# Second attention of a six-stage model: output projection of batch 0 inside its loop, first norm's statistics in the experts' tail, fewer split passes, score stacks filled from SBUF

## The chip, the cores and the metric

The kernel runs on one core of a Trainium2 chip. The metric is the device time of one execution in microseconds (us). The core has five engines with queues of their own: TensorE (PE, with its weight loads as PEld), VectorE (DVE), ScalarE (ACT), GpSimd (POOL) and SyncE (SP), which here only issues DMAs.

## The reference

Six residual steps on x[2, 1024, 128] in f32. The change touches the seams of the fifth, the attention of layer 1, with the fourth and the sixth, which are mixtures of experts:

```python
x = x + 0.5 * _L1_ffn_ref(_layernorm(x), gate_w, Wg, Wu, Wd, Sg, Su, Sd)   # experts, "moe0"
x = x + _L1_attn_ref(_layernorm(x), W_qkv, b_qkv, W_proj, b_proj)         # attention, 16 heads of 8
x = x + 0.5 * _L1_ffn_ref(_layernorm(x), gate_w, Wg, Wu, Wd, Sg, Su, Sd)   # experts, "moe1"

# _L1_attn_ref
scores = q @ k.T / sqrt(8) + slopes[:, None, None] * minimum(idx[None, :] - idx[:, None], 0)
y = softmax(scores) @ v
return y @ W_proj + b_proj
# _L1_ffn_ref: logits = flat_x @ gate_w.T; each of 16 experts takes its 256 best tokens
```

## The kernel before, in words

The 2048 tokens stand as 16 tiles of 128 (a quarter is 4 tiles, one PSUM bank of 512 columns). Every stage is a block in which each engine runs a list written by hand; engines meet through semaphores, and a barrier ends the block. `renew()` clears the semaphores between stages and adds a second barrier.

**Tail of moe0.** The experts' results are scattered with adds into two tensors in DRAM. DVE adds the first to XB (L1254), then the second, quarter by quarter as it comes back (L1258), which gives X. Then comes the barrier.

**Prologue of the attention.** DVE takes mean and variance of 16 tiles (L84, L87), ACT one square root, DVE normalises 16 tiles (L143), PE transposes them and ACT keeps them as XT. PE projects q and k, for batch 0 and then batch 1 (`n` = 0 to 3, L1691). Each projection is split into three bf16 parts, high, middle and low: ACT writes it twice (to F and as the high part, L1594), DVE makes the rest, the middle and the low part (L1622 to L1626). SP sends the parts to DRAM (`keep`, L1517) and reads them back into stacks of rows (`part_rows`, L1502 and L1508): KS and QS, [128 rows, 3 stacks, 4 heads, 1024] in bf16. Rows 0 to 71 are parts, 72 to 119 the bias rows (`first_rows`, `bias_rows`), two more the rows' maxima. A stack serves one step `s`, that is one group of 4 heads and one batch. PE also makes the values V, which DVE copies with the bias.

**The loop.** First 48 chunks (`LEAD`) of raw scores go to PE (L1712), and DVE takes the maximum of each (L1635). Then come 128 units `gu`. Each has four score matmuls (L1727), four more chunks for the maxima of a later step, while there are any (512 in all, so until unit 115), ACT's two exponentials (L1606), on the diagonal a multiplication on POOL (L1578), and the product with the values (L1743). Every 8 units half a step ends: its maxima are split into two rows (L1649, L1651), which SP writes into the stack with 8 small DMAs (`maxima`, L1526), and PE waits for them in `z.mrows`; its outputs are turned and normalised into Y.

**The end.** After the loop a block of its own turns Y, projects it and adds it to X; the stage of moe1 then makes the norm (L84 to L160) and the gate's logits (L1267), and DVE's first step on the logits is L1155.

## Time and profile before

| what | us |
|---|---|
| median of 3 runs (1349.92 to 1354.03) | 1349.97 |
| the profiled execution, its own time | 1347.04 |
| its span, first to last instruction | 1345.3 |
| PE busy in it | 1170.4 |
| DVE busy | 851.5 |
| ACT busy | 697.2 |
| POOL busy | 513.6 |

Times inside the execution count from the start of the span. The mean granted clock of TensorE is 0.922 of its full 2.4 GHz. A row of the timeline gives start, length, engine, line, operation, output and inputs, the number of instructions, and in brackets the idle time before it and what ended it. An f32 matmul of 512 columns shows as two records.

### The profile page before, as it was taken

What the parts mean: (1) busy time and instruction counts of PE and PEld (TensorE: products, weight loads), DVE (VectorE), ACT (ScalarE), POOL (GpSimd) and SP (SyncE); (2) the same over time, 40 slices, a digit from 0 to 9 for tenths busy, and PEclk for the clock granted to TensorE, in tenths of its full rate; (3) what the DMA queues carried; (4) which work ended last, traced back from release to release, by engine and by line L of the source; (5) the groups of instructions that cost most, each with busy time, mean ns of one, the idle gap of its engine ahead of it and who ended that gap; (6) DMA issues with size and microseconds to landing.
All of it is one profiled execution on the core that took longest, in us unless ns stands there. A gap on an engine that the chain in (4) does not pass through costs nothing. (4 is left out here: it accounts for less than half of the span.)

```text
span 1345.3 us, 18773 instructions
## 1 busy us (share of the span) xinstructions
PE 1170.4 (87%) x6259; PEld 579.2 (43%) x6259; DVE 851.5 (63%) x1880; ACT 697.2 (52%) x857; POOL 513.6 (38%) x513
## 2 busy tenths in 40 slices
PE   3899999999999977599458999999999998577884
PEld 1444444444444843499431222222222222446874
DVE  6266576666656467633378788888888880684321
ACT  3577778777788143132140566666666666221221
POOL 0056566665657102278500131231131131034774
PEclk9699999999999977799775899999999999597997
DMA  2000010100101105167568020320220000312662
GB/s 80 1 6 24 25 30 22 32 22 22 38 16 33 33 1 191 19 166 187 107 150 157 5 38 12 48 39 10 48 44 5 1 1 5 129 32 70 169 159 20
DMA packets 57099, 73.89 MB, mean 55 GB/s; under 512 B 21162, under 2 KB 45614, under 8 KB 55214
## 3 DMA queue, kind: packets, MB, share of 16 engines
q1 hardware_dynamic: 42876, 63.91, 18.4%
q0 software_dynamic: 11264, 8.92, 4.6%
q8 instruction: 40, 0.66, 0.2%
q10 hardware_dynamic: 2888, 0.15, 0.1%
q14 instruction: 31, 0.25, 0.1%
HBM read 59.68 MB, written 12.98 MB: 54 GB/s over the span
## 5 line engine op out<-in xcount | busy, mean ns | idle before, releaser
L1635 DVE TENSOR_REDUCE at_MX<-psum 128x1 f32<-128x512 f32 x512 | 318.3, 682 | 60.0 <-PE psum L1712 60.0
L1606 ACT ACTIVATE at_PR<-psum 128x1024 f32<-128x1024 f32 x256 | 251.5, 1022 | 178.3 <-PE psum L1727 178.0
L1578 POOL TENSOR_TENSOR at_PR<-at_PR,at_FAC 128x512 f32<-128x512 f32 x64 | 81.0, 1266 | 344.9 <-ACT at_PR L1606 344.9
L1712 PE MATMUL psum<-at_KS,at_QS 120*128 120x512 bf16 x512 | 205.8, 404 | 7.4 <-DMA at_KS<-at_parts_dram 6.3
L1727 PE MATMUL psum<-at_QS,at_KS 122*128 122x512 bf16 x512 | 192.6, 386 | 4.8 <-DMA at_QS<-at_MR 4.3
L515 ACT ACTIVATE PR<-psum 128x1024 f32<-128x1024 f32 x144 | 140.9, 1026 | 82.2 <-PE psum L799 77.8
L520 ACT ACTIVATE PR<-PR 128x1024 f32<-128x1024 f32 x144 | 144.5, 1062 | 0.0
L799 PE MATMUL psum<-Q,K 64*128 64x512 f32 (+3 forms) x768 | 143.5, 502 | 1.2 <-ACT PR L515 1.2
L1743 PE MATMUL psum<-at_PR,at_VG 128*32 128x512 f32 x1024 | 136.2, 604 | 9.5 <-ACT at_OTS L1600 4.7
L811 PE MATMUL psum<-PR,V 128*64 128x512 f32 (+3 forms) x768 | 139.7, 495 | 0.1
L492 POOL TENSOR_SCALAR_AFFINE_SELECT PR<-PR 128x256 f32<-128x256 f32 (+1 forms) x112 | 57.7, 529 | 173.8 <-ACT PR L520 173.7
L1359 PE MATMUL psum<-moe_XGT,moe_WE 128*128 128x256 f32 x512 | 120.3, 389 | 0.0
L1236 DVE TENSOR_TENSOR moe_H<-moe_GL,psum 128x512 f32<-128x512 f32 x64 | 44.0, 687 | 115.1 <-ACT moe_GL L1131 115.1
L1727 PEld LDWEIGHTS psum<-at_QS,at_KS 122*128 122x128 bf16 x512 | 48.9, 98 | 154.7 <-ACT at_PR L1606 96.3
L1359 PEld LDWEIGHTS psum<-moe_XGT,moe_WE 128*128 128x128 f32 x512 | 98.1, 197 | 12.8
L799 PEld LDWEIGHTS psum<-Q,K 64*128 64x128 f32 x768 | 64.2, 186 | 78.5 <-issue 62.6
L1712 PEld LDWEIGHTS psum<-at_KS,at_QS 120*128 120x128 bf16 x512 | 50.4, 99 | 88.6 <-DVE at_MX L1635 54.2
L1080 POOL DMA_INDIRECT moe_XG<-moe_rows_dram,moe_IDX x64 | 63.5, 993 | 60.4 <-DMA moe_IDX<-moe_LS 41.5
L811 PEld LDWEIGHTS psum<-PR,V 128*64 128x64 f32 x768 | 47.0, 136 | 85.3 <-issue 75.3
L1131 ACT ACTIVATE moe_GL<-psum 128x512 f32<-128x512 f32 x64 | 38.2, 597 | 86.1 <-PE psum L1359 86.1
L434 POOL TENSOR_TENSOR ACC<-ACC,PR 128x128 f32<-128x128 f32 (+3 forms) x64 | 71.5, 1117 | 5.3 <-POOL PR L492 1.0
L434 DVE TENSOR_TENSOR XN<-XN,PR 128x128 f32<-128x128 f32 (+3 forms) x64 | 60.4, 943 | 17.6 <-POOL PR L492 16.7
(222 smaller groups left out, 1546.8 us busy)
## 6 DMA issues: line engine op xcount, KB each, us to landing
moe_WE<-in_c_We SPq DMA_DIRECT2D x32, 768.0 KB, 4.3
XB<-at_r_dram SPq DMA_DIRECT2D x32, 256.0 KB, 3.8
at_QS<-at_parts_dram SPq DMA_DIRECT2D x24, 192.0 KB
at_KS<-in_c_krows SPq DMA_DIRECT2D x8, 384.0 KB
at_parts_dram<-at_SPL SPq DMA_DIRECT2D x12, 256.0 KB, 2.5
moe_rows_dram<-XNS SPq DMA_DIRECT2D x2, 1152.0 KB, 9.0
at_KS<-at_parts_dram SPq DMA_DIRECT2D x16, 128.0 KB
at_QS<-at_MR SPq DMA_DIRECT2D x128, 1.0 KB
```

Of the source, the lines that this page charges most:

```text
L434: eng.tensor_tensor(into, old, PR[second[0]][:, h, second[1]:second[1] + w], ALU.add).then_inc(done, 1)
L515: act.activation(PR[u][:, :, :], S[(b + u) % 2][:, :, :], ACT.Tanh, scale=SCALE0 / CLAMP).then_inc(z.clamped, 1)
L520: act.activation(PR[u][:, :, :], PR[u][:, :, :], ACT.Exp, scale=CLAMP).then_inc(z.exped, 1)
L799: mm = pe.matmul(S[(b + u) % 2][:, h, at:at + w], K[row[h], b, j * P:(j + 1) * P], Q[row[h], b, q:q + w], start=True, stop=True)
L811: mm = pe.matmul(O[row[h], q:q + w], V[:, b, j, row[h]], PR[u][:, h, at:at + w], start=(u < 2), stop=(u >= NU - 2), skip_group_check=True)
L1359: mm = pe.matmul(ps[4 + 2 * m + h][:, j * CAP:(j + 1) * CAP], WE[:, e % DEEP, at:at + P], XGT[:, e % 2, :], start=True, stop=True)
L1578: pool.tensor_tensor(pr, pr, FAC[:, 4 * (s // 2):4 * (s // 2) + 4, :], ALU.mult).then_inc(z.factored, 1)
L1606: act.activation(PR[:, gu % PRS, 2 * r:2 * r + 2, :].rearrange("p h n -> p (h n)"), g.psum[:, 2 * r * BANK:(2 * r + 2) * BANK], ACT.Exp).t ...
L1635: dve.tensor_reduce(MX[:, 4 * (r // 2 % 4) + r // 8, r % 2:r % 2 + 1], bank(("max", c))[:, :], AX, ALU.max).then_inc(z.reduced, 1)
L1712: pe.matmul(bank(("max", c))[:, :], QS[0:MROW, t, h, I * P:(I + 1) * P], KS[0:MROW, t, h, khalf * BANK:(khalf + 1) * BANK], start=True, st ...
L1727: mm = pe.matmul(ps[h][:, :], KS[0:KALL, t, h, J * P:(J + 1) * P], QS[0:KALL, t, h, half * BANK:(half + 1) * BANK], start=True, stop=True)
L1743: mm = pe.matmul(O[32 * h:32 * h + 32, :], VG[:, s % 2, J, h, :], PR[:, gu % PRS, h, :], start=(J == 0), stop=(J == BT - 1), skip_group_ch ...
```

## The change

1. In moe0's tail PE adds the two parts with identity matmuls in PSUM; DVE takes the statistics from PSUM quarter by quarter, ACT copies X and takes the roots, all before the barrier. The prologue starts with the normalisation, shared by DVE and ACT.
2. Each projection is written once by ACT (high part) and once by DVE (the rest, from PSUM); ACT makes the middle part. The factor of q goes into the weights. V's bias is added by POOL.
3. The trip through DRAM is gone. For each part and side, three DMAs of 8 rows each fill the stack from SPL: 18 per step in place of 8 (with the one of the bias rows 19 in place of 9). The stack of step 1 is asked for after the first chunk.
4. Maxima rows go out before the next stack's rows; for the first half ACT issues four of the eight.
5. Output projection, bias, addition and statistics of quarters 0 to 2 are put behind units 117, 119, 124 and 126; the last quarter, the norm and the logits follow the loop in the same block. moe1 starts with its logits made, after `renew()`.

```diff
+                if lanes == 2:
+                    act.activation(MX[:, 0:1], g.eps[:, 0:1], ACT.Sqrt).then_inc(z.table, 1)
+                    for k in range(4):
+                        act.wait_ge(s.stats, 4 * k + 4)
+                        act.activation(g.X[:, 4 * k:4 * k + 4, :].rearrange("p t d -> p (t d)"), ps[4 + k], ACT.Copy
+                                       ).then_inc(z.kept, 1)
+                        norm_root(act, g, s, k)
...
                     for k in range(4):
...
+                        dve.wait_ge(z.resummed, k + 1)
+                        norm_stats(dve, g, s, k, ps[4 + k])
+                        if k:
+                            norm_inverse(dve, g, s, k - 1)
+                    norm_inverse(dve, g, s, 3)
...
+                if lanes == 2:
+                    pe.wait_ge(z.added, 1)
+                    for k in range(4):
+                        pe.matmul(ps[4 + k], g.ident[:, :], g.XB[:, 4 * k:4 * k + 4, :].rearrange("p t d -> p (t d)"),
+                                  start=True, stop=False, skip_group_check=True)
+                    for k in range(4):
+                        pe.wait_ge(z.reloaded[k], 16)
+                        pe.matmul(ps[4 + k], g.ident[:, :], LAST[:, 4 * k:4 * k + 4, :].rearrange("p t d -> p (t d)"),
+                                  start=False, stop=True, skip_group_check=True).then_inc(z.resummed, 1)
...
-STACK_DMAS, STACK_FIRST = 9, 2
+STACK_DMAS, STACK_FIRST = 19, 2
...
+FIRST_OUT, SECOND_OUT = 117, 124
...
+        last_row, last_out = bank(("row", HALVES - 1)), bank(("out", HALVES - 1))
+        proj_bank = [last_out, last_row, last_row, last_row]
+        yturn_bank = [last_out, last_row, last_out, ps[3]]
...
+        def maxima_rows(eng, hs, k):
+            t, half = hs // 2 % STACKS, hs % 2
+            eng.wait_ge(z.msplit, hs + 1)
+            for h in range(4):
+                eng.dma_start(QS[MROW + k:MROW + k + 1, t, h, half * BANK:(half + 1) * BANK].rearrange("o (i n) -> o i n", n=P),
+                              MR[4 * h:4 * h + 4, k, :]).then_inc(z.mrows, 16)
...
                 def part_rows(s):
                     q, b, t = s // 2, s % 2, s % STACKS
...
+                    for k, ready in enumerate((y.high, y.mid, y.split)):
+                        for side, into in enumerate((QS, KS)):
+                            n = 2 * b + side
+                            sp.wait_ge(ready, n + 1)
+                            for r in range(PARTS):
+                                row = PROWS * r + DH1 * (k if side == 0 else (k - r) % PARTS)
+                                sp.dma_start(into[row:row + DH1, t, :, :], SPL[q::QUADS, n, k, :]).then_inc(z.stacks[t], 16)
...
-                for n in range(3):
-                    keep(n)
-                sp.wait_ge(y.kept[0], 2 * 16 * PARTS)
+                first_rows(0)
+                bias_rows(0)
+                sp.dma_start(WP[:, :], g.i["c_Wproj"]).then_inc(y.out, 16)
+                sp.dma_start(HB[:, :], g.i["c_bproj"].partition_broadcast(P)).then_inc(y.out, 16)
                 part_rows(0)
-                keep(3)
-                sp.wait_ge(y.kept[1], 2 * 16 * PARTS)
+                sp.wait_ge(z.maxed, 1)
+                first_rows(1)
+                bias_rows(1)
                 part_rows(1)
                 sp.dma_start(FAC[:, :, :], g.i["c_factor"]).then_inc(z.factors, 16)
                 first_rows(2)
                 bias_rows(2)
-                part_rows(2)
                 for hs in range(HALVES):
                     s = hs // 2 + 2
-                    if hs % 2 and hs >= 3 and s < STEPS1:
+                    maxima_rows(sp, hs, 0)
+                    if hs:
+                        maxima_rows(sp, hs, 1)
+                    if hs == 0:
+                        part_rows(2)
...
+                    if gu % UNITS == 5 and 0 < s <= 4:
+                        pool.wait_ge(y.out, 32)
+                        pool.tensor_tensor(g.X[:, 4 * s - 4:4 * s, :], g.X[:, 4 * s - 4:4 * s, :],
+                                           bcast(HB[:, :].unsqueeze(1), [P, 4, D]), ALU.add).then_inc(z.biased, 1)
...
+                def high(n):
                     act.wait_ge(y.projected, n + 1)
...
+                    act.activation(SPL[:, n, 0, :], g.psum[:, PJ[n] * BANK:(PJ[n] + 2) * BANK], ACT.Identity,
+                                   bias=bq[:, n % 2:n % 2 + 1]).then_inc(y.high, 1)
+                def middle(n):
+                    act.wait_ge(y.rest, n + 1)
+                    act.activation(SPL[:, n, 1, :], F[:, n % 2, :], ACT.Copy).then_inc(y.mid, 1)
...
+                normalised(1)
+                for k in range(2):
+                    norm_keep(act, g, s_, k, ps[k])
+                normalised(3)
+                act.wait_ge(y.bscaled, 2)
+                high(0)
+                norm_keep(act, g, s_, 2, ps[0])
+                high(1)
+                middle(0)
+                norm_keep(act, g, s_, 3, ps[1])
+                middle(1)
+                values(0)
+                high(2)
+                middle(2)
+                values(1)
+                high(3)
+                middle(3)
+                values(2)
+                values(3)
+                act.activation(OTS[:, 0, 0:1], g.eps[:, 0:1], ACT.Exp).then_inc(y.table, 1)
...
+                for k in range(3):
+                    norm_root(act, g, last_norm, k)
                 take(HALVES - 1)
+                norm_apply(act, g, last_norm, 2, g.XNS)
+                act.wait_ge(z.yturned, 4)
+                act.activation(g.XT[:, 3 * BANK:], ps[3], ACT.Copy).then_inc(z.yt_last, 1)
+                norm_keep(act, g, last_norm, 0, ps[0])
+                norm_keep(act, g, last_norm, 1, ps[1])
+                norm_root(act, g, last_norm, 3)
+                norm_keep(act, g, last_norm, 2, ps[0])
+                act.activation(OTS[:, 0, 0:1], g.eps[:, 0:1], ACT.Exp).then_inc(z.table, 1)
+                norm_keep(act, g, last_norm, 3, ps[1])
...
+                def rest(n):
+                    dve.wait_ge(y.high, n + 1)
+                    wait(dve, y.split, n - 1)
+                    dve.scalar_tensor_tensor(out=F[:, n % 2, :], in0=g.psum[:, PJ[n] * BANK:(PJ[n] + 2) * BANK],
+                                             scalar=bq[:, n % 2:n % 2 + 1], in1=SPL[:, n, 0, :], op0=ALU.add,
+                                             op1=ALU.subtract).then_inc(y.rest, 1)
+                def low(n):
+                    dve.wait_ge(y.mid, n + 1)
+                    dve.tensor_tensor(SPL[:, n, 2, :], F[:, n % 2, :], SPL[:, n, 1, :], ALU.subtract).then_inc(y.split, 1)
+                normalised(0)
                 dve.wait_ge(y.loaded, 48)
+                dve.tensor_scalar(W[:, 0:D], W[:, 0:D], SCALE1, None, ALU.mult).then_inc(y.bscaled, 1)
                 dve.tensor_scalar(bq[:, 0:1], bq[:, 0:1], SCALE1, None, ALU.mult).then_inc(y.bscaled, 1)
...
+                normalised(2)
+                for b in range(2):
+                    for n in (2 * b, 2 * b + 1):
+                        rest(n)
+                    for n in (2 * b, 2 * b + 1):
+                        low(n)
...
+                    if gu == FIRST_OUT:
+                        keep_y(0)
+                        keep_y(1)
+                    elif gu == FIRST_OUT + 2:
+                        add_out(0)
+                        add_out(1)
+                        last_stats(0)
+                        last_stats(1)
+                    elif gu == SECOND_OUT:
+                        keep_y(2)
+                    elif gu == SECOND_OUT + 2:
+                        add_out(2)
+                        last_stats(2)
+                for k in range(3):
+                    norm_inverse(dve, g, last_norm, k)
                 normalise(HALVES - 1)
+                for k in range(2):
+                    norm_apply_vector(dve, g, last_norm, k, g.XNS)
+                add_out(3)
+                last_stats(3)
+                norm_inverse(dve, g, last_norm, 3)
+                norm_apply_vector(dve, g, last_norm, 3, g.XNS)
...
+                turn_norm(0)
+                turn_norm(1)
+                pe.wait_ge(y.loaded, 48)
+                pe.wait_ge(y.bscaled, 1)
+                project(0)
+                project(1)
+                turn_norm(2)
+                values(0)
+                turn_norm(3)
+                project(2)
+                project(3)
+                for k in range(1, 4):
+                    values(k)
...
-                pe.wait_ge(y.high, 4)
...
+                pe.wait_ge(y.rest, 4)
                 pe.wait_ge(y.varea, NT // 4)
+                pe.wait_ge(y.out, 32)
                 for c in range(4 * LEAD):
...
+                    if gu == FIRST_OUT:
+                        pe.wait_ge(z.normed, HALVES - 2)
+                        pe.wait_ge(z.reduced, CHUNKS1)
+                        pe.wait_ge(z.msplit, HALVES)
+                        turn_y(0)
+                        turn_y(1)
+                    elif gu == FIRST_OUT + 2:
+                        project_out(0)
+                        project_out(1)
+                    elif gu == SECOND_OUT:
+                        pe.wait_ge(z.normed, HALVES - 1)
+                        pe.wait_ge(z.added, 1)
+                        turn_y(2)
+                    elif gu == SECOND_OUT + 2:
+                        pe.wait_ge(z.added, 2)
+                        project_out(2)
                 multiply(last)
+                pe.wait_ge(z.yt, 3)
                 turn_out(HALVES - 1)
...
+                pe.wait_ge(z.exped, 2 * STEPS1 * UNITS)
+                pe.wait_ge(z.normed, HALVES)
+                turn_y(3)
+                norm_turn(pe, g, last_norm, 0, g.XNS, ps[0])
+                pe.wait_ge(z.added, 3)
+                project_out(3)
+                norm_turn(pe, g, last_norm, 1, g.XNS, ps[1])
+                logits(0)
+                norm_turn(pe, g, last_norm, 2, g.XNS, ps[0])
+                logits(1)
+                pe.wait_ge(last_norm.xt, 2)
+                norm_turn(pe, g, last_norm, 3, g.XNS, ps[1])
+                logits(2)
+                logits(3)
...
         stage_alibi_attention(nc, g, sem)
-        stage_experts(nc, g, sem, "moe1", out, False)
+        renew()
+        stage_experts(nc, g, sem, "moe1", out, True)
```

SP's list in the prologue of the attention, before: the parts go to DRAM (L1517), come back into stack 0 (L1502, L1508), and the last of them follow.

```order
L1517 DMA at_parts_dram<-at_SPL 32x4x1024 x9
L1502 DMA at_QS<-at_parts_dram 24x4096
L1508 DMA at_KS<-at_parts_dram 24x4096
L1502 DMA at_QS<-at_parts_dram 24x4096
L1508 DMA at_KS<-at_parts_dram 16x4096
L1508 DMA at_KS<-at_parts_dram 8x4096
L1502 DMA at_QS<-at_parts_dram 24x4096
L1508 DMA at_KS<-at_parts_dram 8x4096
L1508 DMA at_KS<-at_parts_dram 16x4096
L1517 DMA at_parts_dram<-at_SPL 32x4x1024 x3
```

Now, from the first rows of stack 0 to the first of stack 1 (L1489 to L1493 are the bias rows):

```order
L1489 DMA at_QS<-in_c_qrows 48x4096
L1490 DMA at_KS<-in_c_mones 2x4096
L1493 DMA at_KS<-in_c_krows 48x4096
L1512 DMA at_WP<-in_c_Wproj 128x128
L1513 DMA at_HB<-in_c_bproj 128x128
L1505 DMA at_QS<-at_SPL 8x4x1024 x3
L1505 DMA at_KS<-at_SPL 8x4x1024 x3
L1505 DMA at_QS<-at_SPL 8x4x1024 x3
L1505 DMA at_KS<-at_SPL 8x4x1024 x3
L1505 DMA at_QS<-at_SPL 8x4x1024 x3
L1505 DMA at_KS<-at_SPL 8x4x1024 x3
L1489 DMA at_QS<-in_c_qrows 48x4096
```

A stack's 72 rows of each side, which came in 8 transfers of 8, 16 or 24 rows, come in 18 transfers of 8 rows.

PE's list from the last units of the loop to moe1's first transposes, before:

```order
L1727 MATMUL psum<-at_QS,at_KS 128x512 x4
L1743 MATMUL psum<-at_PR,at_VG 32x512 x12
L1751 MATMUL psum<-ident,at_OTS 128x128 x4
L1487 UNCONDITIONAL_BRANCH
L1795 UNCONDITIONAL_BRANCH
L1800 MATMUL psum<-ident,at_Y 128x128 x16
L1807 MATMUL psum<-at_WP,XT 128x128 x16
L1784 UNCONDITIONAL_BRANCH
L1261 UNCONDITIONAL_BRANCH
L160 MATMUL psum<-ident,XNS 128x128 x16
L1267 MATMUL psum<-gate,XT 128x16 x16
```

And now, from the projection of quarter 2 behind unit 126 to the block's end (L1847 is the turn of the outputs, L1862 that of Y, L126 the norm's):

```order
L1872 MATMUL psum<-at_WP,XT 128x128 x4
L1839 MATMUL psum<-at_PR,at_VG 32x512 x8
L1847 MATMUL psum<-ident,at_OTS 128x128 x4
L1862 MATMUL psum<-ident,at_Y 128x128 x4
L126 MATMUL psum<-ident,XNS 128x128 x4
L1872 MATMUL psum<-at_WP,XT 128x128 x4
L126 MATMUL psum<-ident,XNS 128x128 x4
L1880 MATMUL psum<-gate,XT 128x16 x4
L126 MATMUL psum<-ident,XNS 128x128 x4
L1880 MATMUL psum<-gate,XT 128x16 x4
L126 MATMUL psum<-ident,XNS 128x128 x4
L1880 MATMUL psum<-gate,XT 128x16 x8
```

Behind the loop a quarter of the projection is left on PE, and the norm's transposes and the logits stand between its pieces.

## Rows read from the trace of the kernel before

**Rows 1.** Windows: stretches (us), busy time per engine, clock, DMA share, GB/s.

```profile
674.54:712.26 37.72, 17.65 (x64) 11.52 (x65) 23.65 (x66) 13.63 (x15) 2.41 (x4) 0.73 0.68 162
712.26:744.25 31.99, 28.58 (x49) 5.05 (x50) 29.61 (x52) 0.00 (x0) 0.00 (x0) 0.50 0.73 135
1107.66:1137.99 30.33, 25.81 (x161) 5.92 (x157) 1.75 (x7) 22.41 (x24) 5.09 (x4) 1.00 0.00 1
1137.99:1166.01 28.02, 17.01 (x96) 15.09 (x96) 12.07 (x60) 7.43 (x11) 4.51 (x1) 0.71 0.30 118
```

**Rows 2.** Timeline, end of moe0 and start of the attention, DVE.

```profile
666.16 2.29 DVE L1254 TENSOR_TENSOR XB<-XB,X 128x2048 f32<-128x2048 f32 x1 [10.32 <-DMA X<-moe_sum_dram]
...
671.88 1.49 DVE L1258 TENSOR_TENSOR X<-moe_SG,XB 128x512 f32<-128x512 f32 x2 [1.09 <-DMA moe_SG<-moe_spare_dram]
674.59 0.87 DVE L84 BATCH_NORM_STATS2 stats<-X 128x6 f32<-128x128 f32 x4 [1.21 <-PEq L1841]
```

**Rows 3.** Timeline, f32 matmuls of 512 columns in moe1, PE.

```profile
1171.37 2.06 PE L1282 MATMUL psum<-XT,SGU 128*128 128x512 f32 x2
...
1178.20 1.96 PE L1282 MATMUL psum<-XT,SGU 128*128 128x512 f32 x4
```

**Rows 4.** Windows around the end of moe0 and the projections (columns as in Rows 1).

```profile
655.00:668.00 13.00, 0.19 (x2) 0.00 (x1) 2.45 (x3) 0.00 (x0) 5.57 (x4) 0.62 0.54 106
679.00:684.00 5.00, 4.10 (x16) 2.98 (x17) 4.51 (x18) 1.97 (x4) 0.00 (x0) 0.50 1.03 182
684.00:692.00 8.00, 7.35 (x16) 3.08 (x16) 3.00 (x3) 4.72 (x5) 0.00 (x0) 0.91 0.40 64
```

**Rows 5.** DMA issues of the prologue: count, KB each, us to landing.

```profile
at_bv<-in_c_bv SPq DMA_DIRECT2D x1, 64.0 KB, 5.2
```

**Rows 6.** Timeline, prologue of the attention to its first units.

```profile
675.42 0.42 SPq L1531 DMA_DIRECT2D at_bv<-in_c_bv  x1
...
687.72 1.10 ACT L1594 ACTIVATE at_SPL<-psum,at_bq 128x1024 bf16<-128x1024 f32 x1
...
712.26 19.91 PE L1712 MATMUL psum<-at_KS,at_QS 120*128 120x512 bf16 x34 [6.31 <-DMA at_KS<-at_parts_dram]
...
734.26 5.11 SPq L1526 DMA_DIRECT2D at_QS<-at_MR  x8
...
744.25 1.89 PE L1727 MATMUL psum<-at_QS,at_KS 122*128 122x512 bf16 x4 [2.78 <-DMA at_QS<-at_MR]
```

**Rows 7.** Timeline, front stage's norm and logits and moe0's first step.

```profile
500.86 1.65 ACT L111 ACTIVATE XNS<-X,shift,rdev 128x128 f32<-128x128 f32 x4 [0.32 <-DVE shift L103]
500.96 1.11 DVE L118 TENSOR_SCALAR XNS<-X,moments,rdev 128x128 f32<-128x128 f32 x4
...
503.73 3.59 PE L873 MATMUL psum<-gate,XT 128*128 128x16 f32 x16
...
509.06 0.42 DVE L1155 TENSOR_REDUCE moe_MX<-psum 128x16 f32<-128x256 f32 x1
```

**Rows 8.** Windows: one stack's fill in the loop, and `keep`'s transfers.

```profile
849.30:861.60 12.30, 11.56 (x67) 3.43 (x65) 10.51 (x22) 8.20 (x9) 3.15 (x4) 1.00 0.81 125
694.00:695.00 1.00, 0.42 (x4) 0.23 (x3) 0.97 (x2) 0.36 (x1) 0.00 (x0) 1.00 1.02 383
```

**Rows 9.** Timeline, SP's issues of maxima rows for halves 3 and 4.

```profile
810.86 30.43 SPq L1526 DMA_DIRECT2D at_QS<-at_MR  x16
```

**Rows 10.** Timeline, last units and the block behind the loop.

```profile
1115.65 1.04 PE L1727 MATMUL psum<-at_QS,at_KS 122*128 122x512 bf16 x4 [1.35 <-DMA at_QS<-at_MR]
...
1132.78 1.92 PE L1743 MATMUL psum<-at_PR,at_VG 128*32 128x512 f32 x16
...
1135.54 1.06 PE L1743 MATMUL psum<-at_PR,at_VG 128*32 128x512 f32 x8 [0.85 <-POOL at_PR L1578]
1136.68 0.60 ACT L1600 ACTIVATE at_OTS<-psum 128x512 f32<-128x512 f32 x1 [2.53 <-PE psum L1743]
...
1142.33 3.84 PE L1807 MATMUL psum<-at_WP,XT 128*128 128x128 f32 x32 [0.94 <-DMA at_HB<-in_c_bproj]
```

211 lines of the change are left out of this document (70 added, 141 removed).

## Prediction, written before the changed kernel ran

> **What bounds the kernel now.** I read the windows of the stages first. Between the end of moe0's additions and moe1's first step on its logits, three stretches are seams in which no engine is full: 37.7 us from the attention's start to its first chunk of scores, 32.0 us from there to the first unit, and 28.0 us from the last turn of the outputs to moe1's first step, there with ACT at 7.43 and DVE at 12.07 us of work [rows 1]. The last 20 units (30.3 us) keep PE at 25.8 and ACT at 22.4. The timeline then says what each seam waits for: the first chunk for a DMA into stack 0, and the first unit for the maxima rows [rows 6]. The units between are not touched by the change, except for the DMAs beside them. So the sum has four places.
>
> **1. moe0's tail: +8.0 us to the barrier, then -5 us.** XB is complete at 666.16 + 2.29 = 668.45 [rows 2]. Now eight f32 matmuls of 512 columns follow on PE. One costs 2.06 us at the low clock (1.7 from start to start) and half of 1.96, less its drain, so 0.86, at the high one [rows 3]. PE has been idle since 655.2; the granted clock was 0.62 over 655 to 668 and 0.50 in 679 to 684, so the matmuls start at 1.2 GHz. In the trace the clock came up inside 684 to 692 (0.91 over 8 us is 1.4 us at half), 5.5 us after PE had begun at 679.9 [rows 4]. With denser work I take 4.3 us: 2.5 matmuls slow, 5.5 fast, end at 668.5 + 4.3 + 4.7 = 677.5. Bounds: all fast 675.4, all slow 682.2. DVE takes about 1.1 us of statistics per quarter and 0.35 for an inverse; the first quarter is summed at 674.9, so its fourth statistics end near 680.2, then ACT's copy 0.6, root 0.3, inverse 0.35: 681.3. The barrier costs what it costs now, from 673.37 to 674.59 [rows 2]. New start of the attention: 682.5 instead of 674.5. In return the first normalisation runs at once (it now starts 5 us after the barrier).
>
> **2. Prologue to the first chunk: +5.1 us.** Counted from the start. The bias bv lands 5.2 us after its issue at +0.9, so at +6.1 [rows 5, 6], and the scaled weights of q wait for it; the normalisation (ACT 1.65 us a quarter, DVE 1.11 [rows 7]) and transposes hide in that time. Projection 0 at +6.5, two slow matmuls, +9.9; ACT's high part takes 1.10 [rows 6], +11.05; the first DMA moves data at about +12.1.
>
> Two chains run from there. ACT's own list (four high and four middle parts at 1.05, two kept banks, four value copies at 0.6, with DVE's rests at 1.25 between) ends at +26.8. The other is the fill of stack 0, 18 DMAs of 64 KB into 8 rows each. What does one cost? The trace has no row of such a DMA alone, so I bound it. In the loop a stack's fill (384 KB of bias rows and 8 DMAs of parts, 1.5 MB) took 12.3 us at a DMA share of 0.81 and 125 GB/s, while `keep`, which reads 128 partitions, moved 383 GB/s at the same share [rows 8]. The engines are thus busy at a third of their rate when they write a few rows of SBUF. By bytes a 64 KB DMA would take 0.5 us (64 KB at 125 GB/s). If the rate goes with the rows (24 rows at 125 GB/s, 8 rows at 42), it takes 1.5 us. If each DMA costs the same, whatever its rows, it is 12.3 less 2.6 for the bias rows, over 8: 1.2 us. I take 1.2, because it makes up the row's total from DMAs of 8, 16 and 24 rows alike, and since the share says that it is the writing side that holds.
>
> The Trainium skill, page "SBUF — State Buffer", section "Door 1: The DMA port swizzle", speaks against this change: DMA bandwidth goes with the SBUF ports that the partitions reach, four adjacent partitions share one port, and a port gives about 27 GB/s. By it, as an estimate, 8 adjacent rows reach two ports and 64 KB takes 1.2 us, so a stack 21.7 us; with no such limit it would be 9 us. By that rule, the trace agrees with my middle value.
>
> Nothing overlaps inside the queue, so stack 0 is ready at 12.1 + 18 x 1.2 + 1.2 = +34.9, later than ACT's list. First chunk: 682.5 + 34.9 = 717.4, against 712.26 [rows 6]: **+5.1**. What was saved (passes of ACT and DVE and the way through DRAM) is given back here.
>
> **3. First chunk to first unit: +3.3 us.** It took 32.0 us [rows 1]; PE was through with its 48 chunks 2.8 us before and waited for the eight maxima rows, issued from 734.26 in 5.11 us, behind 20 us of other transfers [rows 6]. Now SP starts stack 1 only after the first chunk, and the maxima rows queue behind it: 1.5 to the first byte, 5.0 for the fixed rows (0.8 MB at 162 GB/s [rows 1]), 21.6 for 18 DMAs, 6 for the factors and stack 2's fixed rows (1.8 MB, between 383 and 162 GB/s, so 4.7 to 11), 1.2 for the rows themselves: 35.3. ACT's issuing of half of them doesn't help, since SP's half stands in line.
>
> **4. The end: -14.6 us.** Behind unit 117 eight transposes of Y (1.1 us) fall before the 1.35 us in which PE waits for the maxima rows of the last half at 1115.65: free; without this cover 1.1. Behind unit 119 eight projection matmuls at 3.84/16 = 0.24 [rows 10] are 1.9 us. PE and ACT take turns there with no slack, and the next score matmuls wait behind them: +1.9. Behind 124, four transposes: +0.5. Behind 126, 1.0 us, hidden: the last product waits for POOL until 1135.54, 0.9 us after PE could have started it. Their addition and statistics let ACT's last root end 0.3 us after the 1136.68 at which it copies the outputs [rows 10]. Sum +2.7.
>
> Behind the last turn of the outputs, from 0: normalise 0.6; turn Y 0.6; ACT keeps it, 1.8; DVE applies quarters 0 and 1 until 2.8 (1.11 each [rows 7]) while PE projects quarter 3 until 2.9; addition 0.7, statistics 1.2, root 0.4, inverse 0.35, apply 1.1: 6.7; the table load for the exponential stands ahead of ACT's last keep, so 7.3 + 0.6 = 7.9; four logits matmuls 0.9; and from the last logits (503.73 + 3.59) to DVE's first step moe0 took 1.74 us, `renew()` included [rows 7]. Together 10.6, where 28.0 stood [rows 1]: -17.4 + 2.7 = **-14.7**, rounded with the uncertain pieces to -14.6.
>
> **In the loop** a fill lasts 2.6 + 21.6 us and starts once the eight maxima rows of an odd half are out. Those of the next half are issued from 25 us after the first (two halves took 30.43 with 5.1 of issue at each end [rows 9]) and are wanted some 36 us after them; the fill is done by 5.1 + 1 + 24.2 = 30.3. Nothing waits. POOL's bias pieces fall into its idle time.
>
> **Sum:** 5.1 + 3.3 - 14.6 = -6.2 us. On the profiled execution's own 1347.04 (span 1345.3) that is 1340.8; the median of the runs is 1349.97, 2.9 above it, so I forecast 1343.8.
>
> **Rivals.**
>
> A. *Few rows cost nothing extra.* The DMA goes by bytes, 0.5 us each. Then ACT's list decides the first chunk (682.5 + 26.8 = 709.3, -3.0) and the maxima rows are there in time (-2.7). -20.3: 1329.7. For it: the two narrow DMAs in each fill of now show no wait of PE in the loop. Against it: 125 against 383 GB/s. Chance 0.25.
>
> B. *Slower.* The rate goes with the rows: 1.5 us each. Place: stack 0, 18 x 0.3 = 5.4 more, and as much again ahead of the maxima rows of the first half; +4.6 in all. In the loop a fill then ends 36 us after the odd half's rows, and the next half's rows, behind it, come up to 1.7 us late, five times. 1354.6 to 1363. It decides from 1.37 us per DMA, where the sum is zero. For it: 12 engines on 24 rows. Against it: then DMAs of 24, 16 and 8 rows would have to take 1.5 each, and 8 of them with the bias rows 14.6 us, not 12.3. Chance 0.12.
>
> C. *No measurable change.* PE stays at 1.2 GHz through the sum in moe0's tail (ends 682.2, +3.2 after the overlap) and in the last pieces behind the loop, where a transposition and logits double (+1.5). -1.5: 1348.5. For it: PE's work there is broken by waits, and the clock was 0.71 over today's end [rows 1]. Against it: it stayed at 1.0 until the loop's end. Chance 0.13.
>
> **How the numbers follow.** My forecast has 0.50; within it the cost of one DMA (18 stand ahead of the first chunk and 18 ahead of the maxima rows, so 0.1 us is 3.6 us) and the tail's clock give 1338 to 1349. A measurement here tells 0.3%, 4 us. Faster by more than that: 0.35 of the forecast's 0.50, all of A, 0.02 of C: 0.62. Within it: 0.13 of the forecast, 0.10 of C and 0.03 of B: 0.26. Slower: 0.02, 0.01 and 0.09: 0.12. The range runs from just under A to the lower end of B: 1327 to 1355.
>
> **What would show it.** First normalisation at 682.5 and X's sum on PE from 668.5; the first chunk behind a DMA of SPL into KS at about 717; PE's first unit waiting for maxima rows some 35 us later; DVE's first step of moe1 28.0 - 17.4 = 10.6 us behind the last turn of the outputs. The forecast is wrong if the DMA windows of the fill show well above 55 GB/s, or if units of the loop wait for a stack.

## The result, and the profile after

| kernel | median us (range, runs) | ratio to the kernel before, 95% interval |
|---|---|---|
| before | 1349.95 (1348.57 to 1354.03, 4) | |
| changed | 1336.41 (1334.17 to 1338.45, 4) | 0.989 [0.987, 0.991] |

The change saves 13.5 us (1349.95 - 1336.41), where 6.2 were forecast. The windows of the changed kernel's trace are the tail of moe0 from DVE's first addition to the attention's start, then start to first chunk, first chunk to first unit, the last units, and the stretch behind the last turn. The last four answer to [rows 1].

```profile
673.12:690.15 17.03, 10.13 (x16) 4.04 (x16) 7.69 (x41) 3.13 (x8) 0.00 (x0) 0.70 0.22 62
690.15:720.13 29.98, 17.02 (x64) 10.21 (x65) 13.57 (x18) 17.16 (x26) 3.18 (x7) 0.73 0.46 79
720.13:749.13 29.00, 28.37 (x49) 5.05 (x50) 28.27 (x50) 0.00 (x0) 0.00 (x0) 0.50 0.65 142
1113.86:1144.19 30.33, 27.84 (x184) 9.95 (x180) 8.56 (x38) 23.45 (x29) 5.11 (x4) 1.00 0.01 1
1144.19:1157.62 13.43, 10.50 (x60) 9.61 (x60) 6.08 (x26) 5.51 (x11) 0.00 (x0) 0.68 0.00 1
```

Laid between the same marks the two profiles give the account below; the last column is a second profile of the changed kernel on another chip (experiment e5).

| stretch (us) | before | changed | difference | forecast | changed again |
|---|---|---|---|---|---|
| DVE's first addition of X to attention start | 8.38 | 17.03 | +8.65 | +8.0 | 15.71 |
| start to first chunk | 37.72 | 29.98 | -7.74 | -2.8 | 29.66 |
| first chunk to first unit | 31.99 | 29.00 | -2.99 | +3.3 | 29.00 |
| first unit to last turn of outputs | 393.08 | 394.43 | +1.35 | +2.7 | 394.17 |
| last turn to moe1's first step on the logits | 28.68 | 14.06 | -14.62 | -17.4 | 14.62 |
| sum | 499.85 | 484.50 | -15.35 | -6.2 | 483.16 |

The tail, in the timeline of PE and DVE: the four matmuls on XB take 6.7 us, the four on the second part 3.6, and DVE stands idle for 7.7.

```profile
675.46 6.70 PE L1354 MATMUL psum<-XB,ident 128*128 128x512 f32 x8 [13.05 <-DVE XB L1223]
682.00 3.60 PE L1358 MATMUL psum<-moe_SG,ident 128*128 128x512 f32 x8
683.12 0.89 DVE L84 BATCH_NORM_STATS2 stats<-psum 128x6 f32<-128x128 f32 x4 [7.72 <-PE psum L1358]
```

The prologue, in the timeline of SP, ACT and PE. It answers to [rows 6]. Three DMAs of 64 KB take SP 1.92 to 2.10 us to issue, 0.64 to 0.70 each, and the last three of stack 0 go out from 712.61. ACT's last copy of the prologue ends at 716.65. The first chunk waits for a DMA. The first unit shows no wait for maxima rows any more: PE goes on from the 48th chunk.

```profile
701.02 2.10 SPq L1505 DMA_DIRECT2D at_QS<-at_SPL  x3
...
712.61 1.92 SPq L1505 DMA_DIRECT2D at_KS<-at_SPL  x3
715.58 1.07 ACT L1591 ACTIVATE at_V<-psum 128x512 f32<-128x512 f32 x2
...
720.13 19.92 PE L1808 MATMUL psum<-at_KS,at_QS 120*128 120x512 bf16 x34 [6.66 <-DMA at_KS<-at_SPL]
...
741.06 8.28 PE L1808 MATMUL psum<-at_KS,at_QS 120*128 120x512 bf16 x14 [0.21 <-DVE at_MX L1675]
749.13 1.91 PE L1823 MATMUL psum<-at_QS,at_KS 122*128 122x512 bf16 x4
```

The last row of the windows has the granted clock at 0.68; the 16 records of the last eight tiles' logits take 3.26 us there, 0.20 each, where the eight of the first four tiles take 1.01, 0.13 each.

```profile
1149.05 1.01 PE L1880 MATMUL psum<-gate,XT 128*128 128x16 f32 x8
...
1152.38 3.26 PE L1880 MATMUL psum<-gate,XT 128*128 128x16 f32 x16
1157.62 0.42 DVE L1124 TENSOR_REDUCE moe_MX<-psum 128x16 f32<-128x256 f32 x1
```

Between the start of the span and DVE's first addition in moe0's tail nothing is changed, and yet that addition starts at 666.16 before, at 673.12 and 660.12 in the two profiles of the changed kernel. So profiles are compared below by stretches between marks (one profile of each kernel), and times by their ratio to the kernel before on the same chip.

### The profile page after: what moved, and what is told of

Read it like the earlier page. It is cut to its first block and busy times, and to the rows that moved or that the text cites. A ratio compares the mean times of both kernels' runs of the same rounds, so it can differ in the third digit from the quotient of the medians.

```text
span 1336.7 us, 18924 instructions
## 1 busy us (share of the span) xinstructions
PE 1179.0 (88%) x6275; PEld 584.1 (44%) x6275; DVE 845.3 (63%) x1874; ACT 705.9 (53%) x883; POOL 520.2 (39%) x540
## 3 DMA queue, kind: packets, MB, share of 16 engines
q1 hardware_dynamic: 44956, 60.76, 17.5%
## 5 line engine op out<-in xcount | busy, mean ns | idle before, releaser
L1330 PE MATMUL psum<-moe_XGT,moe_WE 128*128 128x256 f32 x512 | 125.6, 402 | 7.5 <-ACT moe_XGT L1089 7.5
L1330 PEld LDWEIGHTS psum<-moe_XGT,moe_WE 128*128 128x128 f32 x512 | 101.9, 205 | 22.9 <-issue 8.5
L397 DVE TENSOR_TENSOR XN<-XN,PR 128x128 f32<-128x128 f32 (+3 forms) x64 | 60.4, 943 | 17.7 <-POOL PR L455 16.7
```

Of the source, the lines that this page charges most:

```text
L397: eng.tensor_tensor(into, old, PR[second[0]][:, h, second[1]:second[1] + w], ALU.add).then_inc(done, 1)
L1330: mm = pe.matmul(ps[4 + 2 * m + h][:, j * CAP:(j + 1) * CAP], WE[:, e % DEEP, at:at + P], XGT[:, e % 2, :], start=True, stop=True)
```

## The experiments

All edits start from the changed kernel; "item" in this section is the number in the list of the change. Each ratio is to the kernel before on the same chip; that kernel's medians there were 1338.39 to 1340.3 us. Where a time is said to be "above e5" (the changed kernel again), medians from two chips are compared; by the ratios the differences are 41 us for e2, 13 for e3, 9 for e4 and 44 for e10.

**e1, parts through DRAM.** Undoes item 3's way of filling the stacks. It is not quite the trip of the kernel before: each part goes to DRAM as soon as it is ready.

```diff
-  sp.dma_start(into[row:row + DH1, t, :, :], SPL[q::QUADS, n, k, :])     # 18 per step
+  keep(0); sp.wait_ge(y.kept[0], 2 * 16 * PARTS); part_rows(0); keep(1)  # 6 to DRAM, 8 back
```

> The changed kernel, with the stacks filled as in the kernel before: six DMAs (one for each part and side) take a batch's parts to DRAM as soon as each part is ready, and eight DMAs of 8, 16 and 24 rows bring them back, 9 per step with the bias rows. Theory 1 (the fill from SBUF is cheap: its DMAs go out every 0.65 us and the last lands 5.6 us after the last issue): the trip through DRAM costs the prologue what it cost in the kernel before, some 12 us from the first read to the first chunk, behind a last low part that is ready at +18 and lands in DRAM 2 to 3 us later. Start of the attention to the first chunk: 34 us (32 to 36) instead of 29.98, first chunk to first unit 29.0 unchanged, the rest unchanged: time +4 us against the changed kernel. Theory 2 (what I predicted, 1.2 us for each DMA of 8 rows, so that the trip through DRAM saved nothing): 30 us or less, no difference.

Measured: 1327.92 us, 0.9924 [0.990, 0.9948]. First chunk at +31.36 and first unit 31.29 later. The new fill is worth 1.4 to 1.7 us at the first chunk and 2.3 at the first unit, which in e1 waits for maxima rows (2.08 us). Both theories missed the first chunk (34 and at most 30 us), and the first missed the first unit; but the fill from SBUF does save something, against theory 2. The other 6.4 us by which e1's first chunk is earlier than in the kernel before (37.72 to 31.36) belong to items 1 and 2 and to sending the parts sooner. No run undoes item 2, so its share is not shown.

**e2, halves.** The same bytes in 36 DMAs per step.

```diff
+  for x in range(2):
+      cols = slice(x * BANK, (x + 1) * BANK)
+      sp.dma_start(into[row:row + DH1, t, :, cols], SPL[q::QUADS, n, k, cols])
```

> The changed kernel, with each of the 18 part DMAs of a step cut into two of half the columns: the same bytes to the same rows, 36 DMAs of 32 KB. Theory 1 (SP's issue of 0.65 us per DMA sets the fill): 36 x 0.65 = 23.4 us of issue in place of 11.7; first DMA at +10.9, so stack 0 is there at about +37 and the first chunk comes 37 us after the start instead of 29.98; first chunk to first unit: stack 1, the factors and the fixed rows are issued by +27.5, behind the maxima rows' 22, and their data move as fast as they are issued, so 29 becomes about 32; in the loop nothing waits. Time +9 to +11 us. Theory 2 (the data set it, 0.45 to 0.9 us per 64 KB by what the rows, columns or ports cost): the same bytes take the same time, first chunk at +30 to +31, time within 1 us of the changed kernel.

Measured: 1364.92 us, 1.019 [1.0173, 1.0207], 41 us above e5. First chunk at +36.66, as issue alone gives; first unit 36.95 later (expected 32), after a wait of 7.7 us for maxima rows, and the loop 28.2 us longer (expected 0). Of these 28.2, 18 are further waits for maxima rows; PE's busy time in the loop is 10.3 us longer (388.57 for 378.28 in e5), at a mean granted clock of 0.97 instead of 1.00. SP's issues and PE's waits behind the first unit:

```profile
688.70 4.06 SPq L1507 DMA_DIRECT2D at_QS<-at_SPL  x6
PE psum L1825 <- DMA at_QS<-at_MR: 18.0, 5, 3.9
```

0.65 to 0.68 us per DMA again, for half the bytes: the issue is a price per DMA. A fill of 36 x 0.65 = 23.4 us, the length that my forecast gave it, makes the loop wait.

**e3, maxima rows behind.** Undoes item 4's order on SP.

```diff
-  maxima_rows(sp, hs, 0)  (and 1)      ahead of bias_rows(s), part_rows(s)
+  maxima_rows(sp, hs, 0)  (and 1)      behind them
```

> The changed kernel, with the order of the maxima rows undone: SP issues the next stack's parts first and the maxima rows behind them, as in the kernel before (ACT still issues its four rows of the first half). Theory 1 (the order matters only at the first unit): the fill of stack 2 is 11.8 us of issue from 735.2 on, the first maxima rows then go out at about 747 and land at 751, so the first unit waits some 3 us more: first chunk to first unit 32 us instead of 29.0; in the loop a fill of 12 to 16 us is far less than the 25 us or more that the rows have: no wait. Time +3 us. Theory 2 (my prediction's picture, in which the rows would be late by the whole queue of data, 20 us and more): 36 us or more, and waits for maxima rows in the loop as well.

Measured: 1335.06 us, 0.998 [0.9958, 1.0002], 11 us above e5. First chunk to first unit 33.82 (expected 32), and PE waits 4.62 us at the first unit; the loop is 8.2 us longer, with 6.3 us of waits for maxima rows in four places where I expected none. The order is worth 4.8 + 8.2 us by the profile, 13 in all, as by the ratios.

**e4, projection behind the loop.** Undoes the placement of item 5.

```diff
-  behind units 117, 119, 124, 126: turn_y, project_out, keep_y, add_out, last_stats of quarters 0 to 2
+  multiply(last)
+  turn_y(0); turn_y(1); project_out(0); project_out(1); turn_y(2); project_out(2)   (DVE alike)
```

> The changed kernel, with the output projection of quarters 0 to 2 (turns, keeps, projections, additions, statistics) taken out of the units 117 to 126 and run in one piece behind the last product, ahead of the last turn of the outputs; nothing else is moved. Theory 1 (the pieces in the loop cost the 2.2 us by which units 118 to 127 grew, and behind the loop they stand on the path with all their waits): the last turn comes 2.2 us earlier counted in units but behind a chain of turn 0.6, keep 1.3, project 2, add 1.4, turn, keep, project, 2.5: together 8 to 9 us, and DVE's statistics of three quarters (3.5 us) fall behind it too. From unit 117's scores to moe1's first step on its logits +8 us (6 to 11); time +8. Theory 2 (DVE's and PE's idle time at the end takes them in, as the seam has no full engine): +2 or less.

Measured: 1332.1 us, 0.9945 [0.9928, 0.9963], 8 us above e5; first unit to moe1's first step 415.7 (400.42 + 15.25) against 408.5 and 408.8. That is +7 us, inside theory 1's 6 to 11.

**e5, the changed kernel again.**

> The changed kernel itself, beside the kernels of this group. Both theories: start of the attention to first chunk 30.0 us, to first unit 29.0 more, XB complete plus the tail as in its first profile (start 17.0 us after DVE begins the addition of X; 15.8 to 16.3 in the three variants of it so far). Behind the last turn 14.1 us if PE falls to the low clock in its pieces, 11.9 if it stays at the high one. The points in front of the change (front stage, experts of moe0) may come up to 15 us earlier or later than in its first profile, since nothing of them is changed and they moved so in the other profiles.

Measured: 1324.07 us, 0.9881 [0.9858, 0.9904]. The stretches are in the last column of the table of stretches. All are within 0.6 us of the first profile, except the tail (-1.3), where the clock was 0.82 and not 0.70. The time intervals of e6, e7 and e8 overlap that of e5 (and e9's touches it), so their readings rest on their profiles.

**e6, X's sum on DVE.**

```diff
-  dve.wait_ge(z.resummed, k + 1); norm_stats(dve, g, s, k, ps[4 + k])
+  dve.wait_ge(z.reloaded[k], 16)
+  dve.tensor_tensor(X quarter k, LAST quarter k, XB quarter k, ALU.add); norm_stats(dve, g, s, k)
```

> The changed kernel, with the sum of X in moe0's tail back on DVE: DVE adds the second part to XB quarter by quarter (0.74 us a quarter, two pairs 1.1 us apart for their DMAs) and takes each quarter's statistics from SBUF right behind (1.15 with the inverse of the quarter before 0.3); PE's 8 identity matmuls and ACT's four copies are gone, ACT's roots stay. Theory 1 (the matmuls at 1.2 GHz are what the tail pays: 6.7 us for the first four, 3.6 for the rest, and DVE waits 7.7 us for them): DVE's chain is 0.9 + 4 x 2.15 + 0.8, so the barrier comes 13 us after DVE begins the addition of X instead of 16 to 17; nothing else moves, time -3 to -4 us against the changed kernel. Theory 2 (DVE's statistics and the barrier set it and PE's sum hides ahead of them): no difference, or later by the four additions, +2.

Measured: 1322.13 us, 0.987 [0.9841, 0.9898]. The tail is 12.87 us, as theory 1 had it (-2.8 against e5); the time's 2 us are inside the intervals.

**e7, K side of stack 0 on POOL's queue.** `part_rows(pool, 0, (1,))` beside `part_rows(sp, 0, (0,))`, with a semaphore of its own.

> The changed kernel, with the nine DMAs of the K side of stack 0 issued by POOL instead of SP, as soon as each part is ready; SP issues the nine of the Q side. Theory 1 (SP's issue of 0.65 us each and its wait for K's high part hold the fill): both halves are issued by about +19, and the first chunk waits for ACT's last value copy at +26.5 instead of a DMA: start to first chunk 27 us instead of 30.0. Theory 2 (the data hold it: 0.88 us per DMA whichever queue it comes from, 18 x 0.88 behind the first): 29 to 30 us, no change. Theory 3 (POOL takes well over 1.5 us to issue one): 31 us or more. Stack 1, 2 and the loop are as before, so first chunk to first unit stays 29.0.

Measured: 1321.06 us, 0.9857 [0.9817, 0.9896]. First chunk at +27.80. POOL issued its nine DMAs at 0.54 to 0.60 us each and was done at +19.7, and PE still waited 5.3 us for a DMA, until 8 us after the last issue. Half of the issue gone gives 2 us; what is left is data and landing. Neither theory alone holds (27 and 29 to 30 us).

**e8, bv issued later and waited for by POOL alone** (on top of e6). bv is issued behind the fixed rows of stack 0 with a semaphore of its own; `dve.wait_ge(y.loaded, 32)` stands for 48, and the same on PE.

> The kernel with the sum of X on DVE, and the bias bv issued behind the stacks' fixed rows with a semaphore of its own, so that the weights' scaling and the first projection wait for W and bq alone (POOL alone waits for bv). Theory 1 (what the wait for bv costs is on the path: DVE idles 3.1 us for it and PE's first projection starts 5.85 us after the start): the projection starts once PE has turned its two quarters and ACT has kept them, at +4.6, and the chain high part, DMAs, first chunk moves with it: start to first chunk 28.7 us instead of 30.0, together with the tail -4.5 to -5 us against the changed kernel. Theory 2 (the fill hides it, because SP's last six groups are issue-bound and wait for K's parts): first chunk at 30.0, time as the kernel with the sum on DVE.

Measured: 1320.5 us, 0.9849 [0.9824, 0.9874]. PE's projection starts at +4.69 and the first chunk at +28.91, as in theory 1, but the first unit comes 30.21 later, 1.0 us of it a wait for maxima rows.

**e9, statistics in the prologue.** Undoes item 1.

```diff
-  (moe0's tail) PE's identity matmuls, norm_stats, ACT's copies and roots, norm_inverse
+  (moe0's tail) dve.tensor_tensor(X quarter k, LAST quarter k, XB quarter k, ALU.add)
+  (prologue)    norm_stats 0, 1; norm_inverse 0, 1; normalised(0); norm_stats 2, 3 behind
```

> The changed kernel, with part 1 undone: the sum of X in moe0's tail is DVE's four additions again, and the statistics, roots and inverses of the first norm run at the start of the attention, quarter by quarter (DVE statistics of quarters 0 and 1, their inverses, the normalisation of quarter 0; ACT takes roots and quarter 1; quarters 2 and 3 behind). Theory 1 (the statistics cost nothing in the prologue, since the first projection waits for the landing of bv anyway): the barrier comes 8.4 us after DVE begins the addition of X, as before the change, instead of 15.7 to 17.0; both turned quarters are kept at about +5.9, when the scaled weights are ready at +5.9 too, so start to first chunk 30 to 30.5 us; nothing else moves. Time -7 us against the changed kernel: part 1 costs what it was costed at (+8.0) and brings nothing back. Theory 2 (my prediction's: 5 of the 8 us come back, since the normalisation starts at once): start to first chunk 35 us, time -2 to -3 us.

Measured: 1316.63 us, 0.984 [0.9818, 0.9862]. Tail 8.44, first chunk at +30.56, first unit 29.49 later (0.29 of it a wait for maxima rows). As theory 1 had it, the first chunk is only 0.6 to 0.9 us later than in the changed kernel. The timeline shows that the statistics fit into the time in which bv is on its way, and the projection starts 6.16 us after the start, against 5.87 in the changed kernel (696.02 - 690.15):

```profile
673.85 0.87 DVE L84 BATCH_NORM_STATS2 stats<-X 128x6 f32<-128x128 f32 x4 [1.22 <-PEq L1947]
...
679.53 0.23 DVE L1657 TENSOR_SCALAR at_W<-at_W 128x128 f32<-128x128 f32 x1 [0.66 <-DMA at_bv<-in_c_bv]
...
679.97 4.61 PE L1769 MATMUL psum<-XT,at_W 128*128 128x512 f32 x5 [0.78 <-ACT XT L132]
```

**e10, LEAD 11** in place of 12, and `FIRST_OUT` 118 for 117.

> The changed kernel, with 44 instead of 48 chunks of raw scores ahead of the first unit (LEAD 11 for 12; the first pieces of the output projection behind unit 118 for 117, since the last maxima are taken one unit later). Theory 1 (from the first chunk to the first unit it is DVE's reductions, 48 x 0.60 = 29.0 us, that set the time, not PE or a DMA; the maxima rows land at about +27): first chunk to first unit 26.6 to 27 us instead of 29.0, the loop's length as before, since DVE has idle time in a unit; time -2 us. Theory 2 (the maxima rows come too late, or the four reductions moved into the loop are not free there): 29 us or a loop that is longer by as much; time unchanged or +1.

Measured: 1366.77 us, 1.0207 [1.0183, 1.0232], 43 us above e5, far outside both theories. First chunk to first unit is 29.71, not 27: PE waits 2.89 us for maxima rows there. The loop is 40.0 us longer than e5's, of which 34.1 are waits for maxima rows; the rest is PE's busy time, 6.1 us longer at a mean clock of 0.99. PE's waits in the loop, and the place of one (SP's eight maxima rows, then PE's unit):

```profile
PE psum L1823 <- DMA at_QS<-at_MR: 34.1, 15, 2.6
```
```profile
813.85 5.24 SPq L1473 DMA_DIRECT2D at_QS<-at_MR  x8
820.18 0.39 PE L1823 MATMUL psum<-at_QS,at_KS 122*128 122x512 bf16 x1 [2.57 <-DMA at_QS<-at_MR]
```

The rows are issued by 819.09 and landed by 820.18. With LEAD 12 they have one unit (3.1 us on the mean, 394 us over 128) more than they had here, where they were 2.3 to 2.6 us late. So, as an estimate, the kernel as changed has less than 1 us of slack in every half. Its own trace has one short wait for them in the loop:

```profile
PE psum L1823 <- DMA at_QS<-at_MR: 0.3, 1, 0.3
```

**e11, combined with LEAD 11** (e9, e8's wait, e7, e10).

> All versions that made a seam shorter, together: statistics in the prologue, the wait for bv taken from the projection, the K side of stack 0 issued by POOL, LEAD 11. Theory 1 (the seams add up): tail 8.4 us; start to first chunk 28 us (the data of 18 part DMAs, 13 to 16 us behind the first, hold it; the statistics cost 1.3 us once bv no longer covers them); first chunk to first unit 27 to 28, with some wait for the maxima rows; time -10 us against the changed kernel, ratio to the kernel before 0.980. Theory 2 (the seams hide each other: what is won ahead of the first chunk is lost at the first unit, which waits for the maxima rows behind stack 1's DMAs): -7 us, as with the statistics alone.

Measured: 1351.02 us, 1.0091 [1.0063, 1.0119]. Tail 7.93, first chunk +27.67, first unit 30.75, loop 433.9. Both theories (7 and 10 us faster than the changed kernel) missed: e10's waits are there again (34.2 us, 15), and the first unit waits 3.93 us for maxima rows. Only the tail and the first chunk add up as theory 1 said.

**e12, idle turns.** `pe.transpose(ps[3][:, 0:P], g.ident, g.ident)` 17 times, and 6 times into `ps[4]`: transposes that nobody reads, in PE's waits behind the loop.

> The changed kernel, with 23 turns of the identity matrix added on PE, whose results nobody reads, in its waits behind the loop: 10 behind the last product, 7 behind the last turn of the outputs, 6 behind the second quarter's logits. Theory 1 (PE's waits there let the clock fall to the low level, and the last pieces then take 2 to 3 us more: 14.1 and 14.6 us from the last turn to moe1's first step with the clock at 0.5 to 0.7 in part of it, 11.9 in the profiles in which it stayed at 1.0 until the last logits): the clock stays at 1.0 and the stretch is 11.4 to 12.0 us; up to 1 us of it may go to turns that do not fit into a wait. Theory 2 (the clock there falls whatever PE does, or the stretch is DVE's and ACT's): 13 to 15 us, plus the turns.

Measured: 1325.13 us, 0.9895 [0.9872, 0.9918]: not faster than e5. The stretch behind the last turn in its windows, and the same of e5:

```profile
1133.98:1145.09 11.11, 9.04 (x73) 7.98 (x71) 6.08 (x27) 5.48 (x11) 0.00 (x0) 1.00 0.01 1
```
```profile
1129.29:1143.28 13.99, 10.64 (x60) 10.03 (x60) 6.08 (x26) 5.62 (x11) 0.00 (x0) 0.65 0.00 1
```

At full clock the stretch is 2.9 us shorter. But of the 13 profiles with this block (e4's has more in it) and without idle turns, four have it short too (11.4 to 11.9 us from the start of the turn), and nine are between 12.6 and 15.3; the three with idle turns are 11.3 to 11.7. From the end of that turn to moe1's first step all 16 sort by the clock of the stretch: 10.7 to 11.2 us where it was 0.92 or more, 12.0 and 12.6 at 0.82 and 0.79, 13.4 to 14.2 at 0.68 or less. That the clock costs this is thus shown; that the turns prevent it is likely and not shown, and no time confirms it.

**e13, LEAD 11 with two queues.** `maxima_rows(pool, hs, 1)` behind POOL's work of unit 8 hs - 3, `maxima_rows(sp, hs, 0)` on SP.

> The kernel with LEAD 11, with four of the eight maxima rows of every half issued by POOL (behind its third unit before the half, with a semaphore of their own) and four by SP. Open is what made LEAD 11 lose 40 us in the loop, 15 waits of PE for maxima rows at 2.3 us. Theory 1 (it is SP's issue: eight rows take 5.1 us at 0.64, behind a chain of turn and split of 1.1 us, and the landing 2 us, together 8.5 us, where LEAD 11 leaves two units, 6.2 us): with half of the issue on POOL's queue the rows are out 2.5 us sooner, and the waits fall from 2.3 us each to 0 to 0.5: first unit to last turn 395 to 402 us instead of 434. Theory 2 (the four reductions per unit come too late on DVE, or the data stand in line behind others): the waits stay, 430 us or more. Where POOL's four issues (2 to 2.5 us) stand ahead of a diagonal block, up to 0.6 us per half may come back, 5 us in all.

Measured: 1322.56 us, 0.9863 [0.9835, 0.9892]. First chunk to first unit 27.00, loop 396.55; the waits are gone:

```profile
PE psum L1825 <- DMA at_QS<-at_MR: 0.8, 2, 0.5
```

It is theory 1: e10's 40 us come from SP's issue of eight DMAs of 1 KB in one queue.

**e14 and e15, combined with LEAD 12.** e9, e8's handling of bv, and e12; FAC and the fixed rows of stack 1 ahead of stack 0's parts; e14 with e7's queue, e15 without.

```diff
   first_rows(0); bias_rows(0)
+  sp.dma_start(FAC ...); first_rows(1); bias_rows(1)
   ...
   sp.wait_ge(z.maxed, 1)
-  first_rows(1); bias_rows(1)
   part_rows(1)
-  sp.dma_start(FAC ...)
```

> The combination without LEAD 11: statistics in the prologue, bv waited for by POOL alone, the K side of stack 0 issued by POOL, the idle turns behind the loop; and new: the factors and the fixed rows of stack 1 are loaded ahead of stack 0's parts, when the queue is empty, instead of behind stack 1's, so that the first maxima rows have less data ahead of them. Theory 1 (the seams add up once the first maxima rows don't stand behind data): tail 8.2 us; start to first chunk 27.7; first chunk to first unit 29.0 (48 reductions of DVE); first unit to last turn 394.2; to moe1's first step 11.7: 5 us less than the kernel with the statistics in the prologue alone (which had 8.4, 30.6, 29.5, 394.1, 14.4), ratio to the kernel before 0.980. Theory 2 (the loads ahead delay stack 0, by 1 to 3 us at 0.3 to 0.4 MB per us): first chunk at 30, ratio 0.983.

> The same combination, with all 18 DMAs of stack 0 issued by SP. Theory 1 (issue and data weigh the same here, so POOL's queue gives about what it gave the changed kernel, 2 us): start to first chunk 29.3 to 30, the rest as in the combination with POOL's queue: 2 us more than it. Theory 2 (the data alone hold stack 0): the same time as it.

Measured: e14 1313.87 us, 0.9803 [0.9782, 0.9823]; e15 1313.37 us, 0.9804 [0.9777, 0.9831]. The stretches of e15: 8.30, 27.16, 29.00, 394.05, 11.74; of e14: 8.40, 29.31, 29.00, 393.82, 11.34. The first chunk of e14 came at 29.31 (theories: 27.7 and 30), that of e15 at 27.16 (theories: 29.3 to 30, and the same as e14). The times are equal, as e15's theory 2 said; the first chunk is 2.2 us later with POOL's queue. That e15's is so early comes from the fill. Its first part DMA is issued at +11.16, e9's at +11.15, and e9's first chunk is at +30.56; inside the fill e15 moves 119 GB/s (below). Against e5's 0.9881 they are 0.8% faster, and e15 has the simpler code.

## Why the prediction was wrong

The items are from here on the four places of the prediction's sum.

**The step that failed** is "I take 1.2", the price of a 64 KB DMA into 8 rows, on which items 2 and 3 rest. It took one number for what is two: SP needs 0.65 us to issue one, whatever its bytes (e2), and the data move at a pace of their own, faster than 1.2 us. The first window of the changed kernel holds the first part DMA, alone in the queue (119 GB/s over 0.55 us are its 64 KB). The others lie inside the fills of stack 0, of stack 1 (with fixed rows ahead of it in the queue) and of stack 2:

```profile
702.40:702.95 0.55, 0.55 (x6) 0.45 (x5) 0.00 (x0) 0.00 (x0) 0.00 (x0) 1.00 0.40 119
708.00:718.00 10.00, 4.87 (x29) 3.48 (x27) 5.33 (x5) 7.02 (x9) 1.14 (x4) 0.88 0.54 75
726.00:734.00 8.00, 8.00 (x14) 1.35 (x13) 8.00 (x15) 0.00 (x0) 0.00 (x0) 0.50 0.53 118
748.00:760.00 12.00, 11.71 (x48) 3.45 (x48) 9.70 (x17) 7.86 (x8) 3.82 (x4) 0.78 0.54 73
```

64 KB at 75 and 118 GB/s are 0.87 and 0.56 us. In stack 0 the data are slower than the issue, in stack 1 the issue of 0.65 is the slower of the two. So stack 0 took from its first issue at +10.9 (forecast +11.05) to +29.98, 19.1 us for 18 DMAs with one gap, where 18 x 1.2 + 1.2 and one start of 1 us make 23.8. That is nearly all of the 4.9 us by which the prologue was better than forecast. The bounds 0.5 and 1.5 held; 1.2 was too much. The reading behind it was also off: `keep` ran at a DMA share of 1.02, not at "the same share" as the fill's 0.81 [rows 8], and it writes DRAM, so the two rows say little of what holds a write into a few rows of SBUF. That nothing overlaps in the queue was assumed too; no run tests it by itself. The port rule that I set beside it (the Trainium skill, "SBUF — State Buffer", "Door 1: The DMA port swizzle": as an estimate 54 GB/s for 8 adjacent rows) doesn't agree with the 119 GB/s of the DMA that ran alone, and both paces of the fills lie above it, as the prediction named it for a sign of being wrong. The row for the issue was there: in [rows 6] SP takes 5.11 us to issue eight DMAs of 1 KB, 0.64 each, and I costed the issue of the part DMAs at nothing.

**Item 3** was mis-sized by the same price, 6.3 us (+3.3 forecast, -2.99 measured): the transfers ahead of the maxima rows are short enough, and from the first chunk to the first unit it is DVE that sets the time: 48 reductions at 0.60 us from start to start = 29 us, with DVE at 28.27 of 29.00 in the windows. PE shows 28.37 busy there, but at the same clock (0.50) four score matmuls behind it take 1.91 us, 0.48 each, so PE could go faster. e13 confirms it: 44 chunks, 27.00. What the order of the rows gains is real (e3: 4.8 us there); ACT's half of the issue stands in every run and is not tested.

**"Nothing waits" in the loop** came out nearly true (0.3 us), but for the wrong reason. It was argued with a fill of 24.2 us, and e2 ran about that fill, 23.4 us of issue: 18 us of waits there. What saves the loop is that the issue of a fill takes 12 us. I counted 36 us until rows are wanted; e10 shows that they come less than 1 us before they are wanted.

**Item 1** held as a size: +8.0 forecast, +8.65 and +7.33 measured, with PE at the low clock for its first pass (0.54 in 675.46 to 682.00): four matmuls went slowly where 2.5 were forecast. "Then -5 us" did not: no 5 us came back from it. Moving the statistics back (e9) costs the prologue 0.6 to 0.9 us, since the landing of bv (5.5 us after the start) covers them. Item 1 loses 6 to 7.5 us net by the profiles, 5.5 by the ratios of e5 and e9.

**Item 4** was sized -14.7 and measured -13.3 (+1.35 - 14.62). The pieces in the loop were cheaper than my +2.7. Behind the last turn it is 2.8 us longer than forecast, from the end of that turn 13.43 for 10.6; e12's profile, at full clock, has 11.11 there. The mechanism of rival C was thus in it, with 1.5 us forecast for it.

**Sum.** Forecast -6.2, by profile -15.35 and -16.7, by time -13.5 (the interval is -17.5 to -12.1) and on the other chip -16. Of the 9.1 us between, the prologue has 4.9, the first unit 6.3, the loop 1.4, and tail and end -3.4 together. Rival A's price by bytes alone, 0.5 us, is what the DMA that ran alone took, and near stack 1's 0.56. Stack 0's 0.87 lies halfway to 1.2, so the first chunk stayed behind the end of ACT's list, which was forecast well (+26.8, measured +26.5).

A slip without effect: the "last 20 units (30.3 us)" are 11, by the 44 score matmuls of L1727 in that window.

**Open:** why the data of equal fills move at paces from 72 to 119 GB/s; and what holds ACT in moe0 (below).

## What to carry to other kernels

Price a DMA twice, for the queue that issues it and for the data, and see which ends later; many small DMAs on one queue (here eight of 1 KB, 5.1 us) can be the tightest point of a loop that shows no wait. Before moving work ahead of a barrier, look at what the engines behind the barrier wait for anyway: work that hides under a load there is free, and ahead of the barrier it isn't. Try the large loads ahead of such a train of DMAs, and read its pace anew. Take slack from an experiment that uses it up (one unit less of lead), not from a list of when things are issued.
